# Four graph layers on 32 elements: exponent rows by DMA through DRAM, transposed aggregation for pairs of heads, straight code

## The reference, cut to what matters

```
layer 0: h1, h2, h3 = h@W1, h@W2, h@W3
         relu(softmax(mask(leaky_relu(h1 @ h2.T))) @ h3)
layer 1: q = h@W, 4 heads of 64;  e[i,j] = leaky_relu(e_src[i] + e_dst[j])
         elu(softmax_j(mask(e)) @ q)                     (per head)
layer 2: Q, K, V = h@Wq+bq, ...;  4 heads of 64
         layernorm(softmax(mask(Q K^T / 8)) V @ Wo + bo) * gamma + beta
layer 3: as layer 1, with weights and a of its own for each head
```

## Time and profile before

| | |
|---|---|
| median of 3 runs | 3187.79 us (3183.66 to 3192.85) |
| the profiled execution: its time | 3183.85 us |
| the profiled execution: its span | 3182.1 us |
| TensorE (PE) busy | 3035.8 us, 95% |
| VectorE (DVE) busy | 2168.6 us, 68% |
| ScalarE (ACT) busy | 1629.6 us, 51% |
| GpSimd (POOL) busy | 765.6 us, 24% |
| mean granted TensorE clock | 0.985 |

### The profile page before, as it was taken

One profiled execution on the slowest core, in us unless ns is written; L12 is line 12 of the kernel. 1 busy time (PEld: TensorE's weight loads), 2 busy tenths in 40 slices (PEclk: granted clock), 3 DMA queues, 4 the chain that ended last, 5 costly groups with the idle time before them and its releaser, 6 DMA issues.

```text
span 3182.1 us, 85495 instructions
## 1 busy us (share of the span) xinstructions
PE 3035.8 (95%) x35494; PEld 2287.4 (72%) x35494; DVE 2168.6 (68%) x5660; ACT 1629.6 (51%) x3457; POOL 765.6 (24%) x917
## 2 busy tenths in 40 slices
PE   4799999999999999999999999999999999999985
PEld 2577777777777777777777777777777777777754
DVE  3467767766767766767766767766766766766764
ACT  1355455455555545555545555545555545555533
POOL 1222222222222222222222222222222222222221
PEclk8999999999999999999999999999999999999998
DMA  3000000000000000000000000000000000000000
GB/s 75 14 8 9 15 15 15 8 15 9 15 15 16 8 15 8 16 15 15 9 15 8 15 15 15 8 15 9 15 15 16 8 15 8 16 8 8 2 8 14
DMA packets 38468, 43.75 MB, mean 14 GB/s; under 512 B 2496, under 2 KB 37312, under 8 KB 38048
## 3 DMA queue, kind: packets, MB, share of 16 engines
q1 hardware_dynamic: 37552, 36.97, 3.7%
q0 software_dynamic: 496, 0.92, 0.3%
HBM read 21.11 MB, written 16.78 MB: 12 GB/s over the span
## 4 chain that ended last, share of the span: by engine, by line
PE 90%; ACT 4%; DVE 3%; issue 2%; POOL 0%; SPq 0%; DMA 0%; DVEq 0%; POOLq 0%; ACTq 0%
PE ps L895 19%; PE ps L1000 16%; PE ps L901 11%; PE ps L1051 8%; PE ps L931 7%; PE ps L1026 7%; PE ps L952 7%; PE ps L1035 6%; PE ps L985 4%; PE ps L886 3%; PE ps L940 2%; ACT hn L413 1%; ACT qT L539 1%; DVE stats L629 1%; ACT qx L468 0%
## 5 line engine op out<-in xcount | busy, mean ns | idle before, releaser
L730 DVE SCALAR_TENSOR_TENSOR pA<-ps,gval,adjT 128x512 f32<-128x512 f32 x512 | 358.0, 742 | 209.4 <-PE ps L985 209.4
L413 ACT ACTIVATE hn<-xc,nb,rstd 128x256 f32<-128x256 f32 x384 | 208.4, 592 | 327.4 <-DVE nb L646 327.4
L730 DVE SCALAR_TENSOR_TENSOR pB<-ps,gval,adjT 128x512 f32<-128x512 f32 x512 | 354.4, 740 | 1.0 <-PE ps L1000 1.0
L336 POOL TENSOR_SCALAR rstd<-mv 128x4 f32<-128x4 f32 x160 | 36.7, 229 | 1213.9 <-DVE mv L638 1213.9
L1000 PEld LDWEIGHTS ps<-vals,pA 128*64 128x64 f32 x8192 | 251.0, 138 | 82.1 <-issue 77.5
L1000 PEld LDWEIGHTS ps<-vals,pB 128*64 128x64 f32 x8192 | 249.3, 138 | 82.3 <-issue 57.1
L895 PE MATMUL ps<-wgat,hT 128*128 128x264 f32 x1024 | 272.2, 401 | 8.3 <-DVE pB L783 4.2
L1000 PE MATMUL ps<-vals,pA 128*64 128x65 f32 x8192 | 268.7, 224 | 5.7 <-DVE pA L730 5.7
L349 POOL TENSOR_TENSOR vals<-qx,gval 128x256 f32<-128x256 f32 x256 | 153.8, 622 | 497.8 <-ACT gval L480 497.8
L1000 PE MATMUL ps<-vals,pB 128*64 128x65 f32 x8192 | 267.1, 224 | 5.9 <-DVE pB L730 4.3
L361 POOL TENSOR_TENSOR qx<-qx,xc 128x512 f32<-128x512 f32 x128 | 163.2, 1275 | 364.6 <-ACT qx L489 364.6
(11 more groups left out here) (136 smaller groups left out, 6102.6 us busy)
## 6 DMA issues: line engine op xcount, KB each, us to landing
x_in<-in_x SPq DMA_DIRECT2D x32, 512.0 KB, 3.8
out_x<-xc SPq DMA_DIRECT2D x32, 512.0 KB, 4.0
pX<-in_adj SPq DMA_DIRECT2D x1, 1024.0 KB, 5.8
pX<-in_L_gnn_W SPq DMA_DIRECT2D x2, 256.0 KB, 6.5
pA<-in_L_gnn_a POOLq DMA_DIRECT2D x8, 64.0 KB, 11.7
w<-in_L_gnn_W SPq DMA_DIRECT2D x1, 256.0 KB, 8.2
wgat<-in_L_gnn_W SPq DMA_DIRECT2D x1, 256.0 KB, 9.9
wgat<-in_L_gnn_W SPq DMA_DIRECT2D x2, 128.0 KB, 13.4
```

What stands on the lines that cost most here:

```text
L413: nc.scalar.activation(hn[s][:, t, :], src[:, t, :], ACT.Identity if norm == "in" else ACT.Relu, bias=nb[s][:, t:t + 1], scale=rstd[s][:, ...
L730: last = nc.vector.scalar_tensor_tensor(out=gat_p[s][h % 2][:, t, :], in0=ps[:, BANK[f"R{g}.{h}"], :], scalar=gval[s][:, 1, t, h:h + 1], i ...
```

## The change

- The exponent rows of the graph layers are no longer made on TensorE. gat_row_exp puts the exponents of all heads and tiles (128x16) into grow; one transpose (gat_rows) makes it 16x128, gat_rows_out (VectorE) copies it to SBUF, and spread on SyncE's queue writes it to a DRAM tensor and, when that has landed, loads it back twice with a broadcast to all partitions, two heads into qT and two into hT of the element (two DMAs of 512 KB). gat_weights reads its rows from there.
- Layer 2's aggregation is turned around: the values of a head (64 columns) are stationary, the transposed weights of 512 columns move, and two heads go to the two halves of the output partitions; the result is already transposed for o_rows. The division is by a full matrix: inverse_sums2 writes reciprocals, each repeated 64 times, inverse_spread transposes them on TensorE, inverse_out copies them, norm2 multiplies. o_columns and o_transposed go.
- The hardware loop is gone: 34 slots of straight code on every engine.
- The orders of all engines and the table of banks are others; plus_beta, the transposes of layer 1's input, its first q_rows and part of layer 2's weights stand in other slots.

```diff
-        gval = sets("gval", [P, 3, NT, H])
+        gval = sets("gval", [P, 2, NT, H])
+        grow = sets("grow", [P, H, NT])
+        growT = sets("growT", [H * NT, P])
...
+        gat_r = [[qT[s][:, 0, :], qT[s][:, 1, :], hT[s][:, 0, :], hT[s][:, 1, :]] for s in range(SETS)]
+        r_dram = {g: [nc.dram_tensor(f"r_dram{g}_{s}", [H * NT, P], f32).ap() for s in range(SETS)] for g in (1, 3)}
...
-            slot(Work(0), None, None)
-            slot(Work(1), Work(0), None)
-            with eng.Fori(0, ROUNDS) as i:
-                for j in range(SETS):
-                    slot(Work(j + 2, i), Work(j + 1, i), Work(j, i))
-            slot(None, Work(B - 1), Work(B - 2))
-            slot(None, None, Work(B - 1))
+            for n in range(B + 2):
...
+            def spread(w, g):
+
+                if w is None:
+                    return
+                s, rows_dram = w.s, r_dram[g][w.s]
+                rT_out[g].wait(sp, w)
+                sp.dma_start(rows_dram, growT[s][:, :]).then_inc(r_written[g].sem, 16)
+                r_written[g].wait(sp, w, 16)
+                for dst, first in ((qT[s], 0), (hT[s], 2)):
+                    src = rows_dram.rearrange("(o h t) p -> o h (t p)", o=1, h=H)[:, first:first + 2, :]
+                    sp.dma_start(dst[:, :, :], src.broadcast_to([P, 2, N])).then_inc(r_loaded[g].sem, 16)
+
+            def slot(a, b, c, more=True):
+                if more:
+                    load_next(a)
+                store(c); spread(a, 1); spread(b, 3)
...
+            def gat_row_exp(w, g):
+                if w is None:
+                    return
+                s = w.s
+                gexp_ready[g].wait(act, w, 3)
+                nc.scalar.activation(grow[s][:, :, :].rearrange("p h t -> p t h"), gexp[s][:, 1, :, :],
+                                     ACT.Exp).then_inc(grow_ready[g].sem, 1)
...
-                if h == 3:
+                if h == 3 and t == 1:
...
+            def inverse_out(w, p):
+                if w is None:
+                    return
+                invp_ready.wait(act, w, p + 1)
+                nc.scalar.copy(kT[w.s][:, p, :], ps[:, BANK[f"RB{p}"], :]).then_inc(inv_ready.sem, 1)
+
+            def slot(a, b, c, d):
+                exp2(c, 2, 2); inverse_out(c, 0); exp2(c, 3, 2); q_out(b, 1, 1); exp2(c, 3, 3)
+                exp2(c, 2, 3); normalised(a, 0, 0); normalised(a, 0, 1); weights_out2(c, 3, 1)
...
+            def gat_rows_out(w, g):
+                if w is None:
+                    return
+                rT_ready[g].wait(dve, w)
+                nc.vector.tensor_copy(growT[w.s][:, :], ps[0:H * NT, BANK[f"RT{g}"], 0:P]).then_inc(rT_out[g].sem, 1)
...
                 if ts[0] == 0:
-                    r_ready[g].wait(dve, w, h + 1)
-                    gval_ready[g].wait(dve, w, 1)
+                    if h == 0:
+                        r_loaded[g].wait(dve, w, 32)
+                        gval_ready[g].wait(dve, w, 1)
...
-                        out=gat_p[s][h % 2][:, t, :], in0=ps[:, BANK[f"R{g}.{h}"], :],
+                        out=gat_p[s][h % 2][:, t, :], in0=gat_r[s][h],
...
-            def norm2(w, h):
-                if w is None:
-                    return
-                s = w.s
-                agg2_ready.wait(dve, w, h + 1)
-                nc.vector.reciprocal(rinv[s][:, h, :], rowsum[s][:, h, :]).then_inc(rinv2.sem, 1)
-                rinv2.wait(dve, w, h + 1)
-                nc.vector.tensor_tensor(
-                    hn[s][:, :, h * D:(h + 1) * D],
-                    ps[:, BANK[f"G2.{h}"], 0:NT * D].rearrange("p (t d) -> p t d", t=NT),
-                    rinv[s][:, h, :].unsqueeze(2).broadcast_to([P, NT, D]), ALU.mult).then_inc(agg2_norm.sem, 1)
+            def inverse_sums2(w, p):
+                if w is None:
+                    return
+                s = w.s
+                p2_ready[2 * p].wait(dve, w, NT)
+                p2_ready[2 * p + 1].wait(dve, w, NT)
+                sums = rowsum[s][:, 2 * p:2 * p + 2, :].rearrange("p h t -> p t h")
+                nc.vector.reciprocal(kT[s][:, p, :].rearrange("p (t h d) -> p t h d", t=NT, h=2),
+                                     sums.unsqueeze(3).broadcast_to([P, NT, 2, D])).then_inc(rinv2.sem, 1)
+
+            def norm2(w, p):
+                if w is None:
+                    return
+                agg2_ready.wait(dve, w, p + 1)
+                inv_ready.wait(dve, w, p + 1)
+                nc.vector.tensor_tensor(qT[w.s][:, p, :], ps[:, BANK[f"G2.{p}"], :], kT[w.s][:, p, :],
+                                        ALU.mult).then_inc(oT_ready.sem, 1)
 
             def o_out(w):
                 if w is None:
@@ -810,32 +844,33 @@
...
+            def slot(a, b, c, d):
+                statistics(a, 0); mean_and_variance(a, 0); weights_out2(c, 2, 1); gat_max_t(b, 1)
+                shift_of_norm(a, 0); gat_max(b, 1); norm2(c, 0); weights_out2(c, 3, 0); inverse_sums2(c, 1)
+                gat_shift(b, 1); weights_out2(c, 3, 2); weights_out2(c, 2, 3); gat_rows_out(b, 1)
+                norm2(c, 1); o_out(c); statistics(c, "in"); mean_and_variance(c, "in")
+                gat_weights(b, 1, 0, 0, 1, 2); shift_of_norm(c, "in"); masked_max0(a, 0)
+                gat_weights(b, 1, 0, 3); lrelu0(a, 0); masked_max0(a, 1); times_gamma(c)
+                gat_weights(b, 1, 1, 0, 1, 2); masked_max0(a, 2); gat_weights(b, 1, 1, 3); statistics(c, 3)
...
-            def gat_rows(w, g, h):
-                if w is None:
-                    return
-                if h == 0:
-                    gval_ready[g].wait(pe, w, 2)
-                for t in range(NT):
-                    last = nc.tensor.transpose(
-                        ps[:, BANK[f"R{g}.{h}"], t * P:(t + 1) * P],
-                        gval[w.s][:, 2, t, h:h + 1].broadcast_to([P, P]), ident[:, :])
-                last.then_inc(r_ready[g].sem, 1)
+            def gat_rows(w, g):
+                if w is None:
+                    return
+                grow_ready[g].wait(pe, w)
+                nc.tensor.transpose(ps[0:H * NT, BANK[f"RT{g}"], 0:P], grow[w.s][:, :, :].rearrange("p h t -> p (h t)"),
+                                    ident[:, :]).then_inc(rT_ready[g].sem, 1)
 
...
-            def aggregate2(w, h):
-                if w is None:
-                    return
-                s = w.s
-                if h == 0:
+            def inverse_spread(w, p):
+
+                if w is None:
+                    return
+                rinv2.wait(pe, w, p + 1)
+                for t in range(NT):
+                    cols = slice(t * P, (t + 1) * P)
+                    last = nc.tensor.transpose(ps[:, BANK[f"RB{p}"], cols], kT[w.s][:, p, cols], ident[:, :])
+                last.then_inc(invp_ready.sem, 1)
+
+            def aggregate2(w, p):
+
+                if w is None:
+                    return
+                s = w.s
+                if p == 0:
                     v2_ready.wait(pe, w)
-                pT2_act[h].wait(pe, w, 2)
-                pT2_dve[h].wait(pe, w, 2)
-                for t in range(NT):
-                    for j in range(NT):
-                        for half in range(2):
-                            lo, hi = half * HALF, (half + 1) * HALF
-                            last = nc.tensor.matmul(
-                                ps[lo:hi, BANK[f"G2.{h}"], t * D:(t + 1) * D],
-                                probT2[s][h][:, t, j * P + lo:j * P + hi],
-                                vals[s][:, j, h * D:(h + 1) * D],
-                                start=(j == 0), stop=(j == NT - 1))
+                for h in (2 * p, 2 * p + 1):
+                    pT2_act[h].wait(pe, w, 2)
+                    pT2_dve[h].wait(pe, w, 2)
+                for j in range(NT):
+                    for hh in range(2):
+                        h = 2 * p + hh
+                        last = nc.tensor.matmul(
+                            ps[hh * D:(hh + 1) * D, BANK[f"G2.{p}"], :],
+                            vals[s][:, j, h * D:(h + 1) * D],
+                            probT2[s][h][:, :, j * P:(j + 1) * P],
+                            start=(j == 0), stop=(j == NT - 1))
                 last.then_inc(agg2_ready.sem, 1)
...
+            def slot(a, b, c, d):
+                masked2[1].wait(pe, c, 6); weights_transposed2(c, 1, 0)
+                masked2[1].wait(pe, c, 8); weights_transposed2(c, 1, 1)
+                qx_ready[1].wait(pe, b, 1); weights_transposed2(c, 1, 2)
+                gnorm[3].wait(pe, d, 4); weights_transposed2(c, 0, 2); weights_transposed2(c, 1, 3)
+                weights_transposed2(c, 0, 3)
+                pT2_dve[0].wait(pe, c, 1); q_rows(b, 1, 2)
+                pT2_act[1].wait(pe, c, 1); weights_transposed2(c, 2, 0)
+                pT2_dve[1].wait(pe, c, 1); weights_transposed2(c, 2, 1)
+                pT2_act[0].wait(pe, c, 2); inverse_spread(c, 0); q_rows(b, 1, 3); aggregate2(c, 0)
```

(36 more changed lines are left out.)

183 lines of the change are left out of this document (54 added, 129 removed), and 17 rows, old and new, of the table BANK.

## The result

| | before | after |
|---|---|---|
| median | 3185.89 us (3183.66 to 3192.85, 4 runs) | 3325.51 us (3324.35 to 3328.01, 4 runs) |
| profiled execution: time, span | 3183.85, 3182.1 us | 3326.25, 3324.4 us |
| mean granted TensorE clock | 0.985 | 0.967 |

The change makes the kernel slower: the ratio of the times is 1.0435, with a 95% interval of 1.0417 to 1.0454. The forecast was 3085 us.

What follows compares the result with a forecast made beforehand. TensorE, busy 93.46 of 93.85 us per slot, was taken as the bound. Fill 202 + 29 x 91.2 (2645) + tail 232 = 3079; 1.8 more gave 3081, and 3.9 to the median 3085 us; own range 3060 to 3115, whole 3055 to 3205.

Steps and rivals of the forecast that it cites:

- the 91.2 of the sum: Forecast time of one slot in us: TensorE's 90.5 plus about 0.7 of new stall, taken for 29 slots.
- the tail: The end of the span after the regular slots: 225.4 us in the kernel before, forecast at 232.
- TensorE's work: TensorE's work per element: changes summing to -3.3 us, a slot of 90.5 us (bounds 90.0 and 97.0) without waits.
- Straight code, -36 us: Loop removed on all engines: nine back edges of 4.0 us each go; streaming 34 slots priced at nothing.
- The spread, hidden: SyncE's write and broadcast loads, 7.6 to 11.4 us, hidden behind about 12 us (layer 1) and 9 us (layer 3).
- The reciprocal: inverse_sums2's 128x512 reciprocal on VectorE, twice per element, priced at 0.7 us like any 512-wide operation.
- the rival: Slow wide reciprocal in inverse_sums2, 32%: 2.4 to 4.1 us each, stalling TensorE; time 3132 to 3231 us.
- gat_weights reading SBUF instead of PSUM is priced at nothing: VectorE's weight rows, reading their row factor from SBUF, were taken to cost no extra time.
- about 0.7 us of new stall: Per slot, TensorE reaches gat_aggregate(b,1,1) after 11.7 us while VectorE needs 12.3 us up to gat_weights(b,1,1,3).
- R: Cause named after the profile: inverse_sums2's wide reciprocal on VectorE; removing it was expected to save 70 us.
- C: Cause named after the profile, without a forecast rival: VectorE contending with GpSimd; removing it was expected to save 150 us.
- the signs named for a wrong forecast: Slots over 92.5 us, with TensorE waiting at inverse_spread or gat_rows (reciprocal), gat_aggregate (spread, VectorE's order), or nothing (block price).

Runs made afterwards that it cites:

- e3: The changed kernel with the small reciprocal, residual2 moved from GpSimd to VectorE and plus_beta last in GpSimd's slot: 3172.04 us, ratio 0.9962.
- e4: The kernel before with only its hardware loop written out as 34 slots of straight code: 3148.62 us, ratio 0.9887.
- e1: The changed kernel with the wide reciprocal replaced: eight sums are inverted, then a VectorE copy spreads them: 3215.69 us, ratio 1.0096.
- e2: The changed kernel, wide reciprocal kept, with residual2 moved from GpSimd to VectorE and plus_beta to the end of GpSimd's slot: 3327.27 us, ratio 1.0451.
- e5: The kernel before, loop kept, with gat_weights reading its row factor from hT in SBUF instead of PSUM: 3299.45 us, ratio 1.0363.

## Why the prediction was wrong

The forecast was 3085 us and the kernel took 3325.5, 240 us more. In the profiled execution slots 2 to 31 took 98.97 us on average against the 91.2 of the sum, 7.8 us times 29, and the tail 252.0 us against 232. Of the 7.8 us, 2.7 are the wait for gat_weights above the 0.7 that was forecast, 2.5 the waits behind the reciprocal and 0.9 the half clock; the rest is smaller waits and about a microsecond more of TensorE's work. The steps in their order:

- *TensorE's work* (3.3 us less): right within half a microsecond. The 3.3 us off the 93.46 busy in a slot before make 90.2; a slot of e3 at full clock has 90.66. (The 90.5 of the text still holds the 0.4 idle of that slot.) The block of aggregate2 took 3.59 us against 3.65 taken, so the halves run side by side. Each pair of records advances by 0.43 us, as one full-width record does. The Trainium skill's figure for three tiles ("TensorE: Matmul & The Clock Gate", Part 3), from which the prediction estimated 4.3, does not carry over to these two halves: the trace has 3.59.
- *Straight code, -36 us*: right, 36 us in e4.
- *The spread, hidden*: right. Write and loads land 1.4 and 4.9 us after their issue, 6.3 together and under the lower bound of 7.6; gat_weights waited for them three times in the whole execution (19.7 us, at the ends), not in the slots between.
- *The reciprocal* was priced at 0.7 us, **the first wrong term**: 3.34 us, 6.5 ns an element, inside the 2.4 to 4.1 us of the rival. The rival's working held in the main. By its rule 3.34 us stall 2.4 us a slot at the second reciprocal (all over 0.9) and 0.8 at the first (all over 2.5), 3.3 in all; the waits of gat_rows, inverse_spread and aggregate2 are 1.9 + 0.4 + 0.25, less than that and mostly at gat_rows, not at aggregate2. With the slower clock and the longer ends that follow, it was worth 110 us (e1). The rows of 4 elements allowed both prices, and with that the text chose the cheap one. The rule of the Trainium skill that it quoted ("VectorE: DVE Perf Modes", an iterative divide with a repeat count of 8) pointed to the dear one, and the trace agrees in direction: 6.5 ns an element, against 1.2 from start to start of a plain copy of 512 (0.60 us).
- *"gat_weights reading SBUF instead of PSUM is priced at nothing"*: **the step that failed**. It had no bounds and no rival. It put both wide operands in SBUF while residual2, plus_beta and gat_residual work on GpSimd. In the step "about 0.7 us of new stall" VectorE's 12.3 us grew by 2.6: three rows took 4.16 instead of 1.98, and the leaky relu 1.11 instead of 0.66. 0.7 + 2.6 is 3.3, and the stall measured 3.4. The order was followed rightly; two durations in it were wrong. The 0.45 of the leaky relu do not come from the moved operand: its operands were in SBUF before too, and the new order puts it beside gat_values. The Trainium skill has this rule, in "SBUF — State Buffer", "Who interferes with whom": a VectorE instruction with two inputs in SBUF contends with a GpSimd instruction that reads SBUF, and the page calls their shared ports an exclusive lock. The trace agrees, with one row of 2.83 us between two of 0.74. Read for the operand that moved, it would have added the missing rival.
- *The clock* was left out. After 3.4 us without work the next block took 2.83 us on average in after instead of 2.09 (19 of the 27 blocks between 300 and 2900 us were slow), and the scores behind a slow block took up to 3.05 instead of 1.98. TensorE was busy 91.3 us in a slot at full clock, 92.2 or 93.2 in the others: 0.9 us a slot on average on top of the waits.

e3, with both edits, is still 3172 - 3085 = 87 us over the forecast. Its slots take 94.13 us on average, 2.9 over the 91.2, which is 85 us over 29 slots. Of the 2.9, VectorE's list makes 1.8: two waits of 1.31 + 1.23 us where 0.7 was forecast. The second wait is about as long as residual2, 1.21 us, which VectorE took over; in e1, where it is on GpSimd, that wait is absent between the ends. Half a microsecond is TensorE's own work; the rest is smaller waits and a few slow blocks.

**The causes do not add up**: the edit for R alone gives 110 us (e1), the edit against C alone nothing (e2), both 153 (e3). In the kernel before, C costs 115 by itself (e5). What C costs in the changed kernel is not shown by one number: e3 moved a part of it, and paid for that with work on VectorE.

Of the signs named for a wrong forecast, slots over 92.5 us came, with the waits of gat_rows and inverse_spread that stood for the reciprocal. gat_aggregate came too, which stood for the spread or VectorE's order; that a longer duration of gat_weights would show at the same place was not named.

## What to carry to other kernels

When an operand moves from PSUM to SBUF, look at what GpSimd does at that moment, not only at the bytes: here a VectorE row with two wide SBUF operands took 2.83 us instead of 0.74 beside GpSimd's addition. Moving GpSimd's work elsewhere only helps if nothing that is waited for stands at the new place. Invert the few sums first and spread them afterwards (0.62 us), rather than the spread matrix (3.34). And since in-order lists hand lateness on, price an edit by the sum of the list ahead of the next wait, and try it with the other causes removed, as the same edit gave nothing in e2 and 44 us in e3. A part that can stand by itself, here the straight code, is worth running alone first: it was the fastest kernel.
